# Gated cross-attention block: the rounded numbers of batch 6 transposed on TensorE, batch 7's sums and tokens kept elsewhere, 88 idle transposes

## The chip, the cores and the metric

The kernel runs on one core of one Trainium2 chip. The metric is the device time in microseconds (us), median of several runs; lower is better. The kernel before takes 510.13 us (three runs, 509.61 to 510.55).

## The reference

For each of 8 batches of 512 tokens by 256 channels (all float32):

```python
a   = layernorm(x)                                  # batch b
emb = a + ctx
q, k, v = emb @ wq + bq, emb @ wk + bk, emb @ wv + bv
w   = pos_bias * (|i - j| < 64)                     # 512 x 512, near the diagonal
ek, ew = exp(k - max_k), exp(w - max_w)
y   = sigmoid(q) * (ew @ (ek * v)) / (ew @ ek)
n1  = layernorm(y @ wo + bo + emb) * gamma + beta
n2  = layernorm(relu(n1 @ w1 + b1) @ w2 + b2 + n1) * gamma + beta
x1  = x + tanh(g_xattn) * n2
n3  = layernorm(x1)
xq  = round(n3 * 127 / max|n3|)                     # per token, then scaled back
h   = silu(xq @ Wg) * (xq @ Wu)                     # Wg, Wu, Wd rounded to -1, 0, 1 times a scale
out = x1 + tanh(g_ffn) * (round(h * 127 / max|h|) @ Wd)
```

The hidden width of both feed-forward parts is 1024.

## The kernel before, in words

One function writes a separate instruction list for each engine, by hand, with a semaphore count for every kind of step. Tokens of a batch lie as 4 tiles of 128; `b` is the batch, `t` a token tile, `p` a pair of tiles, `m` one of 8 slices of the hidden width. The batches are staged: while TensorE does the attention of batch b+1 it also does the first feed-forward part of batch b (`hidden`, `feed_forward`) and the rounded part (`gate`, `up`, `down`) of batch b-1. Each engine runs its list in order, and a step whose semaphore isn't there holds all behind it.

Float32 products are made of three TensorE products of rounded halves (`product`, L2502): high by high, high by low, low by high. So between two products ScalarE rounds the high half (`..._upper`) and VectorE subtracts to get the low one (`..._lower`). The table `BANK` says which of the 8 PSUM banks each step of each batch writes; `bank_wait` makes TensorE wait for the last reader of what was in that bank before. `gate` and `up` take two neighbouring banks.

The start. TensorE waits for the identity and then runs `WARM_UP` idle transposes into bank 7 (L2690), then `emb_rows(0, ...)` (L2510, transposes of the embedded tokens, after GpSimd's `embed`, L564), `keys_T` (L2519), `queries`, `keys_values`, the transposed positions (L2469), `attend` (L2562), `key_sums` (L2571) and `attend_far` (L2579). VectorE's list there holds `wkv_lower` (L1518), `emb_lower` (L1609), `key_max` (L1616), `position_max`, `add_bias`, `weighted` (L1644) and `e_lower` (L1649). After `attend_far(0, ...)` come `beta_w1` and `emb_rows(1, 0)`, which waits for bank 7 until VectorE's `b1_whole` (L1567), behind the divisions of batch 0 (`inverse`, L1658).

The rounded part of a batch. For each pair of tiles: GpSimd's `rsqrt` (L554 to L559), ScalarE's `normalise(b, 3, p)` (L870), VectorE's `token_max` (L1711) and `token_scales` (L1719, L1723), ScalarE's `token_quantise` (L943). The rounded tokens must be transposed: for most batches ScalarE writes them as bf16 (`xq_whole`, L961) and SyncE's queue issues a DMA transpose (`xq_rows`, L345). For the batches in `PE_BATCHES`, batch 7 alone, TensorE transposes float16 halves of the same words (`xq_rows`, L2643) and ScalarE copies them out of PSUM (`xq_columns`, L969). Then `gate` and `up` on TensorE (L2662), `silu` on ScalarE (L977), `product` (L1732) and `product_scale` (L1738 to L1750) on VectorE, `quantise` on GpSimd for even tiles (L608, L609) and on ScalarE for odd ones (L982). The rounded products are transposed in the same two ways: `hq_whole` (ScalarE, L999) with a DMA transpose (L352), or TensorE's `hq_rows` (L2652) with ScalarE's `hq_columns` (L990). Then `down` on TensorE (L2684) and `output` on VectorE (L1756), and SyncE stores pairs of tiles (L331).

The sum x1 has one home for all batches, `x1`, and `n3` and the results share `out_t`. So GpSimd's `first_sum(7, p)` (L603) waits for outputs of batch 6, which still read x1. `second_residual` (L1705) adds the result of the first feed-forward part; batch 7 alone does that part in two halves of tokens (`HALVED`: `hidden(7, m, p, HALF[p])`, `feed_pair`), and `second_residual(7, 1)` needs `feed_pair(7, 7, 1)`. The waits of the sums and tokens stand in `first_sum`, `normalise` and `output`.

Of the kernel before, what the change touches and what calls it, by code (L numbers as in the profile page):

```python
# [30 lines left out]
WARM_UP = 50  # L31

PE_BATCHES = (7,)
# [15 lines left out]
    ("embT", 0): (0, 7, 6, 5, 0, 4, 0, 4), ("embT", 1): (1, 3, 7, 0, 7, 6, 7, 6), ("kT", 0): (2, 1, 1, 5, 3, 3, 3, 0),  # L49
# [3 lines left out]
    ("num", 0): (1, 6, 5, 3, 3, 3, 3, 0), ("den", 0): (6, 4, 0, 0, 4, 0, 4, 6), ("num", 1): (3, 3, 1, 7, 6, 7, 6, 1),  # L53
# [31 lines left out]
def flamingo_layer(nc, x, ctx_in, g_xattn, g_ffn, wq, bq, wk, bk, wv, bv, wo, bo, pos_bias, gamma, beta,  # L85
                   w1, b1, w2, b2, w_gate, w_up, w_down, out):
    with ExitStack() as stack:
# [700 lines left out]
        def _(act):  # L788
# [74 lines left out]
            def normalise(b, n, p):  # L863
# [3 lines left out]
                if n == 3:  # L867
                    wait(act, out_stored[p], b, 0)
# [2414 lines left out]
```

## Time and profile before

| | |
|---|---|
| median of 3 runs | 510.13 us (509.61 to 510.55) |
| the profiled execution | 511.8 us, of which its span (first to last instruction) 509.8 us |
| TensorE busy | 480.8 us, 94% of the span |
| VectorE busy | 437.8 us, 86% |
| ScalarE busy | 375.3 us, 74% |
| GpSimd busy | 248.2 us, 49% |
| mean granted TensorE clock | 0.968 of full |
| chain that ended last | TensorE 86%, VectorE 5%, DMA 3%, ScalarE 2% |

TensorE's records overlap, since matmuls are pipelined: a matmul of 128 x 256 shows 0.28 us, and 54 in a row take 6.36 us. So start to start is what counts, not the length of one record. Times in the rows are in us from the start of the span.

### The profile page before, as it was taken

How to read it: one execution, taken by the hardware profiler on the slowest of the kernel's cores; microseconds unless marked ns; L12 is line 12 of the kernel's file. 1: busy time of each engine (PE TensorE's matmuls, PEld its weight loads, DVE VectorE, ACT ScalarE, POOL GpSimd, SP SyncE). 2: the span in 40 equal slices, each digit the busy share in tenths (PEclk: the TensorE clock that was granted, in tenths of full speed). 3: DMA queues.
4: the chain of work that ended last, by engine and by line, in shares of the span. 5: the costliest groups of instructions: out<-in, count | busy, mean ns of one | idle time of the engine just before them, and what ended most of it. 6: DMA issues, size and time to landing. Idle time of an engine off the chain costs nothing.

```text
span 509.8 us, 9743 instructions
## 1 busy us (share of the span) xinstructions
PE 480.8 (94%) x3010; PEld 397.1 (78%) x3010; DVE 437.8 (86%) x1002; ACT 375.3 (74%) x611; POOL 248.2 (49%) x389
## 2 busy tenths in 40 slices
PE   6898999999999999999999999999999999899483
PEld 6687888988877987788877987788878987787242
DVE  6889988786989899898989898999899888769574
ACT  3474869957778788696878688687768596898573
POOL 7292364169234493248525474339225903664511
PEclk9797999999999999999999999999999999999588
DMA  5853252222202331222312330223023101532301
GB/s 185 187 207 125 42 166 84 41 44 84 62 1 53 78 108 35 42 63 73 95 21 63 89 99 1 44 62 113 13 42 84 54 12 22 82 74 52 82 1 42
DMA packets 69329, 36.02 MB, mean 71 GB/s; under 512 B 47008, under 2 KB 68768, under 8 KB 69280
## 3 DMA queue, kind: packets, MB, share of 16 engines
q1 hardware_dynamic: 68448, 35.41, 27.5%
q8 instruction: 25, 0.41, 0.3%
q14 instruction: 24, 0.20, 0.1%
q10 hardware_dynamic: 832, 0.00, 0.1%
HBM read 20.46 MB, written 4.19 MB: 48 GB/s over the span
## 4 chain that ended last, share of the span: by engine, by line
PE 86%; DVE 5%; DMA 3%; ACT 2%; issue 2%; POOL 1%; SPq 0%; DVEq 0%; POOLq 0%; ACTq 0%
PE ps L2502 52%; PE ps L2662 10%; PE ps L2562 9%; PE ps L2684 5%; PE ps L2571 3%; PE ps L2519 2%; PE ps L2510 2%; DMA work<-in_L_xattn_wo_dram 2%; DMA w_bit<-place_c 1%; DVE cols L1738 1%; PE ps L2579 1%; PE ps L2597 1%; DVE work L1732 1%; PE ps L2536 1%; DVE ps L1658 1%
## 5 line engine op out<-in xcount | busy, mean ns | idle before, releaser
L554 POOL TENSOR_TENSOR mv<-mv,cols 128x2 f32<-128x2 f32 x64 | 13.1, 204 | 169.5 <-DVE mv L1604 169.3
L2502 PE MATMUL ps<-w_hi,h_hi 128*128 128x256 f32 x256 | 76.0, 297 | 0.0
L2502 PE MATMUL ps<-w_lo,h_hi 128*128 128x256 f32 x256 | 71.5, 279 | 0.0
L2502 PE MATMUL ps<-w_hi,h_lo 128*128 128x256 f32 x256 | 71.5, 279 | 0.0
L931 ACT ACTIVATE h_hi<-ps,cols 128x512 fp32r<-128x512 f32 (+1 forms) x72 | 45.4, 636 | 12.4 <-PE ps L2502 11.3
L2502 PE MATMUL ps<-n1T_hi,w_hi 128*128 128x512 f32 (+1 forms) x144 | 54.1, 376 | 0.4 <-DVE n1T_lo L1687 0.3
L1658 DVE RECIPROCAL ps<-ps 128x512 f32<-128x512 f32 x16 | 53.7, 3358 | 0.2 <-PE ps L2579 0.2
L2502 PE MATMUL ps<-n1T_hi,w_lo 128*128 128x512 f32 (+1 forms) x144 | 53.3, 370 | 0.0
L2502 PE MATMUL ps<-n1T_lo,w_hi 128*128 128x512 f32 (+1 forms) x144 | 53.3, 370 | 0.0
L2502 PEld LDWEIGHTS ps<-w_hi,h_hi 128*128 128x128 f32 x256 | 48.3, 189 | 3.0 <-DVE h_lo L1693 0.3
L977 ACT ACTIVATE work<-ps,cols 128x1024 f32<-128x1024 f32 x32 | 35.6, 1113 | 20.1 <-DVE work L1732 10.2
L2502 PEld LDWEIGHTS ps<-w_lo,h_hi 128*128 128x128 f32 x256 | 48.3, 189 | 1.1
L1693 DVE TENSOR_TENSOR h_lo<-ps,h_hi 128x512 fp32r<-128x512 f32 (+1 forms) x72 | 43.6, 622 | 5.9 <-ACT ps L936 5.2
L2502 PEld LDWEIGHTS ps<-w_hi,h_lo 128*128 128x128 f32 x256 | 48.2, 188 | 0.0
L2684 PE MATMUL ps<-wdT,w_bit 128*128 128x256 bf16 x256 | 35.9, 287 | 11.5 <-DMA w_bit<-place_c 7.5
L870 ACT ACTIVATE work<-work,nmr,rstd 128x256 f32<-128x256 f32 x64 | 34.8, 592 | 14.3 <-POOL nmr L559 14.3
L557 POOL TENSOR_TENSOR rstd<-mv,cols 128x2 f32<-128x2 f32 x64 | 45.0, 704 | 0.0
L936 ACT ACTIVATE ps<-ps,cols 128x512 f32<-128x512 f32 (+1 forms) x72 | 43.7, 611 | 0.0
L1732 DVE TENSOR_TENSOR work<-work,ps 128x1024 f32<-128x1024 f32 x32 | 38.9, 1215 | 4.9 <-PE ps L2662 3.1
L1596 DVE BATCH_NORM_STATS2 st<-work 128x6 f32<-128x256 f32 x96 | 36.1, 413 | 5.8 <-POOL work L603 5.5
L2684 PEld LDWEIGHTS ps<-wdT,w_bit 128*128 128x128 bf16 x256 | 24.0, 102 | 21.5 <-DMA w_bit<-place_c 10.8
L1738 DVE TENSOR_REDUCE cols<-work 128x1 f32<-128x1024 f32 x32 | 38.7, 1210 | 0.3
(179 smaller groups left out, 1480.6 us busy)
## 6 DMA issues: line engine op xcount, KB each, us to landing
x_in<-in_x_dram SPq DMA_DIRECT2D x16, 256.0 KB, 2.8
emb<-in_ctx_dram SPq DMA_DIRECT2D x16, 256.0 KB, 2.9
work<-in_x_dram SPq DMA_DIRECT2D x8, 512.0 KB, 4.0
out_dram<-work SPq DMA_DIRECT2D x16, 256.0 KB, 2.2
work<-in_L_xattn_w_dram SPq DMA_DIRECT2D x2, 1024.0 KB, 8.7
work<-in_L_ffn_w_gate_dram SPq DMA_DIRECT2D x1, 1024.0 KB, 5.7
work<-in_L_ffn_w_up_dram SPq DMA_DIRECT2D x1, 1024.0 KB, 5.7
place_c<-in_L_ffn_w_down_dram SPq DMA_DIRECT2D x1, 1024.0 KB, 9.0
```

Of the source, the lines that this page charges most:

```text
L557: pool.tensor_tensor(rstd[:, n, c], mv[:, n, c, 1], minus_half[:, c], ALU.pow).then_inc(power_step[n].sem, 1)
L931: nc.scalar.activation(h_hi[:, m % RING, c], h_bank(b, m, p)[:, c], ACT.Relu, bias=b1_col[:, m:m + 1]).then_inc(h_hi_ok.sem, 1)
L936: nc.scalar.activation(h_bank(b, m, p)[:, c], h_bank(b, m, p)[:, c], ACT.Relu, bias=b1_col[:, m:m + 1]).then_inc(h_relu_ok.sem, 1)
L1596: nc.vector.bn_stats(st6[:, n, t, :], src[:, t, :]).then_inc(stats[n].sem, 1)
L1658: nc.vector.reciprocal(bank(b, "den", h), bank(b, "den", h)).then_inc(rden_ok.sem, 1)
L1693: nc.vector.tensor_tensor(h_lo[:, m % RING, c], h_bank(b, m, p)[:, c], h_hi[:, m % RING, c], ALU.subtract).then_inc(h_lo_ok.sem, 1)
L1732: nc.vector.tensor_tensor(prod[t % 2].rearrange("p (a n) -> p a n", a=2), sg.rearrange("p (a n) -> p a n", a=2), bank_pair(b, "up", t), AL ...
L1738: nc.vector.tensor_reduce(hm[:, t:t + 1], prod[t % 2], AX.X, ALU.max, apply_absolute_value=True).then_inc(hm_ok.sem, 1)
L2502: last = nc.tensor.matmul(dst, lhsT, rhs, start=(i == 0 and not begun), stop=(i == n - 1 and ends))
L2562: nc.tensor.matmul(dst, lhsT[:, j, c], rhs[:, j, 0:n], start=(i == 0 and j == 0), stop=False, skip_group_check=True)
L2662: last = nc.tensor.matmul(dst[:, c, :].rearrange("p (j n) -> p j n", n=P), xqT[:, t, k, :], w[:].rearrange("p (j k) n -> p j k n", k=ND)[: ...
L2684: last = nc.tensor.matmul(bank(b, "down", t)[:, 0:D].rearrange("p (k n) -> p k n", n=P), hqT[t % 2][:, k, :], wdT[:].rearrange("p (k j) n ...
```

## The change

1. `WARM_UP` goes from 50 to 88, so 38 more idle transposes of the identity stand before `emb_rows(0, 0)`.
2. `PE_BATCHES` goes from (7,) to (6, 7). Batch 6's two `xq_rows` and four `hq_rows` leave SyncE's queue and become TensorE transposes (2 x 4 and 4 x 8); `xq_whole` and `hq_whole` become `xq_columns` and `hq_columns`.
3. Batch 7's x1 lives in `x_in`, its n3 in `emb`. So `first_sum(7, p)` waits for `emb_ok` instead of batch 6's outputs, and `output(7, t)` waits for the store of batch 6. The wait of `hout` for outputs of the batch before is by tile.
4. The lists of batches 6 and 7 get a new order on all engines, and some steps of batches 0 to 5 change place. `beta_w1` is cut in four pieces, called one after another.
5. A new `BANK` table.

```diff
-WARM_UP = 50
-PE_BATCHES = (7,)
+WARM_UP = 88
+PE_BATCHES = (6, 7)
...
+        def sum_of(b):
+            return x_in if b == NB - 1 else x1
+        def n3_of(b):
+            return emb if b == NB - 1 else out_t
...
             def first_sum(b, p):
...
-                wait(pool, out_ok, b, 2 * p - 2)
-                pool.tensor_tensor(half(x1, p), half(n2, p), half(xb, p), ALU.add).then_inc(x1_ok.sem, 1)
+                if b == NB - 1:
+                    wait(pool, emb_ok, b, 2)
+                else:
+                    wait(pool, out_ok, b, 2 * p - 2)
+                pool.tensor_tensor(half(sum_of(b), p), half(n2, p), half(xb, p), ALU.add).then_inc(x1_ok.sem, 1)
...
-                wait(dve, out_ok, b, 0)
+                wait(dve, out_ok, b, t - NT + 1)
...
+                if b == NB - 1:
+                    wait(dve, out_stored[t // 2], b, 0)
```

SyncE's list loses `xq_rows(6, 0)`, `xq_rows(6, 1)` and `hq_rows(6, 0)` to `hq_rows(6, 3)`. On GpSimd `rsqrt(7, 2, 0)` now stands before `quantise(6, 0)`, and `quantise(6, 2)` after `first_sum(7, 1)`. The end of TensorE's new list:

```diff
+            xq_rows(6, 0)
             hidden(7, 3, 1, HALF[1])
             hidden(7, 4, 1, HALF[1])
             feed_pair(7, 7, 0)
+            hidden(7, 5, 1, HALF[1])
             feed_pair(7, 0, 1)
             gate(6, 0)
+            hidden(7, 6, 1, HALF[1])
+            hidden(7, 7, 1, HALF[1])
+            feed_pair(7, 1, 1)
             up(6, 0)
...
+            xq_rows(6, 1)
             feed_pair(7, 2, 1)
             feed_pair(7, 3, 1)
...
+            gate(6, 1)
             feed_pair(7, 4, 1)
+            feed_pair(7, 5, 1)
             gate(6, 2)
...
             feed_pair(7, 6, 1)
+            hq_rows(6, 0)
+            feed_pair(7, 7, 1)
             gate(6, 3)
             down(6, 0)
...
+            up(6, 1)
+            up(6, 2)
+            up(6, 3)
+            hq_rows(6, 1)
             down(6, 1)
+            hq_rows(6, 2)
+            xq_rows(7, 0)
             down(6, 2)
...
             gate(7, 0)
+            hq_rows(6, 3)
             up(7, 0)
             gate(7, 1)
             up(7, 1)
+            down(6, 3)
             xq_rows(7, 1)
```

VectorE's new list from there: `second_residual(7, 1)`, `tile_stats` (7,3,0), (7,2,2), (7,2,3), (7,3,1), `mean_variance(7, 2, 1)`, `output(6, 0)`, `mean_variance(7, 3, 0)`, `product(6, 1)` with its scale, `product(6, 2)`, `token_max(7, 0)`, `product_scale(6, 2)`, `token_scales(7, 0)`, `product(6, 3)`, `tile_stats(7, 3, 2)`, `product_scale(6, 3)`, `output(6, 1)`, `tile_stats(7, 3, 3)`, `mean_variance(7, 3, 1)`, `output(6, 2)`, `token_max(7, 1)`, `token_scales(7, 1)`, `product(7, 0)` with its scale, `output(6, 3)`, `product(7, 1)`; from there as before.

## Rows read from the trace of the kernel before

**Rows 1.** Stretches: busy (instructions) of TensorE, its loads, VectorE, ScalarE, GpSimd; granted clock, DMA.
```profile
10.00:20.00 10.00, 4.96 (x15) 4.01 (x16) 6.56 (x8) 5.11 (x9) 3.65 (x6) 0.66 0.81 195
...
240.00:250.00 10.00, 10.00 (x68) 9.05 (x67) 9.97 (x17) 9.07 (x19) 6.31 (x4) 1.00 0.43 118
...
470.00:480.00 10.00, 4.00 (x24) 2.45 (x23) 7.11 (x21) 6.77 (x10) 7.24 (x13) 0.70 0.44 96
480.00:490.00 10.00, 7.95 (x31) 3.11 (x28) 4.98 (x16) 6.04 (x13) 2.46 (x5) 0.62 0.08 28
```

**Rows 2.** The chain that ended last, its pieces: start, us, what.
```profile
442.27 6.36 PE ps L2502 x54
...
455.15 1.74 PE ps L2662 x8
...
476.35 3.04 DMA w_bit<-place_c
```

**Rows 3.** The idle transposes, grouped, in the stretches 1.6 to 5 and 7 to 9.6.
```profile
L2690 PE MATMUL ps<-ident 128*128 128x128 f32 x16 | 3.7, 421 | 1.6 <-POOL ident L617 1.6
...
L2690 PE MATMUL ps<-ident 128*128 128x128 f32 x24 | 2.8, 273 | 0.0
```

**Rows 4.** TensorE in order of time at the start (idle time before it, releaser).
```profile
1.61 8.00 PE L2690 MATMUL ps<-ident 128*128 128x128 f32 x50 [1.61 <-POOL ident L617]
14.35 1.94 PE L2510 MATMUL ps<-ident,emb 128*128 128x128 f32 x8 [4.74 <-POOL emb L564]
16.98 2.07 PE L2519 MATMUL ps<-embT_hi,wkv_hi 128*128 128x512 f32 x4 [0.69 <-ACT embT_hi L884]
...
44.27 1.94 PE L2510 MATMUL ps<-ident,emb 128*128 128x128 f32 x8 [1.24 <-DVE cols L1567]
```

**Rows 5.** VectorE in order of time at the start.
```profile
16.96 0.69 DVE L1609 TENSOR_TENSOR embT_lo<-ps,embT_hi 128x512 fp32r<-128x512 f32 x1 [0.16 <-ACT embT_hi L884]
...
19.09 0.69 DVE L1616 TENSOR_REDUCE cols<-ps 128x1 f32<-128x512 f32 x1 [0.16 <-PE ps L2519]
...
27.60 0.76 DVE L1644 TENSOR_TENSOR ps<-ps,kv_f 128x256 f32<-128x256 f32 x2 [0.62 <-ACT ps L897]
...
32.72 1.28 DVE L1649 TENSOR_TENSOR e_lo<-ps,e_hi 128x512 fp32r<-128x512 f32 x2
```

**Rows 6.** TensorE in order of time near the end.
```profile
470.22 0.28 PE L2502 MATMUL ps<-w_hi,h_lo 128*128 128x256 f32 x1
...
475.45 1.89 PE L2684 MATMUL ps<-wdT,w_bit 128*128 128x256 bf16 x8 [2.94 <-DMA w_bit<-place_c]
...
489.47 0.38 PE L2643 MATMUL ps<-ident_h,work 128*128 128x128 f16 x4 [0.20 <-DVE work L1732]
493.10 0.61 PE L2652 MATMUL ps<-ident_h,work 128*128 128x128 f16 x8
```

**Rows 7.** VectorE, GpSimd, then ScalarE, in order of time near the end.
```profile
483.38 0.75 DVE L1596 BATCH_NORM_STATS2 st<-work 128x6 f32<-128x256 f32 x2 [1.54 <-POOL work L603]
487.03 0.69 DVE L1711 TENSOR_REDUCE cols<-work 128x2 f32<-128x512 f32 x1 [2.51 <-ACT work L870]
...
488.11 1.22 DVE L1732 TENSOR_TENSOR work<-work,ps 128x1024 f32<-128x1024 f32 x1
...
491.32 1.21 DVE L1732 TENSOR_TENSOR work<-work,ps 128x1024 f32<-128x1024 f32 x1
...
482.02 1.27 POOL L603 TENSOR_TENSOR work<-work 128x512 f32<-128x512 f32 x1 [2.40 <-DVE work L1756]
...
490.57 0.67 ACT L969 ACTIVATE xqT<-ps,cols 128x512 bf16<-128x512 f16 x1
...
494.76 1.23 ACT L982 ACTIVATE work<-work,cols 128x1024 f32<-128x1024 f32 x1
```

**Rows 8.** Shorter stretches, columns as in rows 1.
```profile
474.00:476.00 2.00, 0.55 (x3) 0.43 (x4) 1.36 (x7) 1.97 (x2) 1.45 (x3) 0.51 0.78 199
...
488.00:490.00 2.00, 1.65 (x10) 0.56 (x8) 1.97 (x3) 1.80 (x5) 0.00 (x0) 1.00 0.00 0
```

More of the change, by code:

```diff
@@ L504, in _ @@
             store(5, 1)
-            xq_rows(6, 0)
             fetch_x_again(7)
-            xq_rows(6, 1)
-            hq_rows(6, 0)
-            hq_rows(6, 1)
-            hq_rows(6, 2)
             store(6, 0)
-            hq_rows(6, 3)
             store(6, 1)
@@ L772, in _ @@
             x_beta(7)
+            rsqrt(7, 2, 0)
             quantise(6, 0)
-            rsqrt(7, 2, 0)
-            quantise(6, 2)
             n2_gamma(7, 0)
@@ L781, in _ @@
             first_sum(7, 1)
+            quantise(6, 2)
             rsqrt(7, 3, 1)
@@ L863, in normalise @@
             def normalise(b, n, p):
-                dst, src = {0: (xn, x_in), 2: (n2, a2), 3: (n3, x1)}[n]
+                dst, src = {0: (xn, x_in), 2: (n2, a2), 3: (n3_of(b), sum_of(b))}[n]
                 wait(act, nmr_ok[n], b, p + 1)
-                if n == 3:
+                if n == 3 and b == NB - 1:
+                    wait(act, embT_ps, b, 2)
+                    wait(act, embo_ok, b, 1)
+                elif n == 3:
                     wait(act, out_stored[p], b, 0)
@@ L1139, in _ @@
             normalise_tile(2, 1)
+            silu(0, 1)
             normalise_tile(2, 2)
-            silu(0, 1)
             normalise_tile(2, 3)
@@ L1421, in _ @@
             hidden_whole(6, 6)
+            silu(5, 0)
             hidden_upper(6, 7)
             hidden_whole(6, 7)
-            silu(5, 0)
             silu(5, 1)
@@ L1479, in _ @@
             hidden_whole(7, 5, 1, HALF[1])
+            xq_columns(6, 1)
             hidden_upper(7, 6, 1, HALF[1])
@@ L1483, in _ @@
             hidden_whole(7, 7, 1, HALF[1])
-            hq_whole(6, 0)
+            silu(6, 1)
+            normalise(7, 2, 0)
+            hq_columns(6, 0)
+            normalise(7, 2, 1)
             silu(6, 2)
+            normalise(7, 3, 0)
             quantise(6, 1)
-            hq_whole(6, 1)
             silu(6, 3)
-            normalise(7, 2, 0)
-            hq_whole(6, 2)
-            quantise(6, 3)
-            hq_whole(6, 3)
-            normalise(7, 2, 1)
-            normalise(7, 3, 0)
+            hq_columns(6, 1)
             product_scales(7, 0)
             token_quantise(7, 0)
+            hq_columns(6, 2)
+            quantise(6, 3)
             xq_columns(7, 0)
@@ L1499, in _ @@
             silu(7, 0)
+            hq_columns(6, 3)
             token_quantise(7, 1)
+            silu(7, 1)
             product_scales(7, 1)
-            silu(7, 1)
             xq_columns(7, 1)
@@ L1927, in _ @@
             weighted(2, 1)
+            weighted(2, 2)
             e_lower(2, 0)
-            e_lower(2, 1)
             hidden_lower(1, 0)
@@ L1932, in _ @@
             tile_stats(0, 3, 1)
+            e_lower(2, 1)
+            e_lower(2, 2)
             hidden_lower(1, 1)
@@ L1936, in _ @@
             tile_stats(0, 3, 3)
-            weighted(2, 2)
             mean_variance(0, 3, 1)
-            e_lower(2, 2)
             add_bias(2, 3)
@@ L2448, in _ @@
             product_scale(7, 0)
+            output(6, 3)
             product(7, 1)
@@ L2478, in far_row, with beta_w1 @@
                 last.then_inc(far_ps, 1)
-            def beta_w1():
+            def beta_w1(piece):
                 pe.wait_ge(load["vectors2"], 16 * VECTORS2)
                 pe.wait_ge(load["w1"], 16)
-                once_bank_wait(B1_BANK, (b1_ok, 1))
-                for m in range(NH):
+                if piece == 0:
+                    once_bank_wait(B1_BANK, (b1_ok, 1))
+                for m in range(2 * piece, 2 * piece + 2):
                     for k in range(ND):
@@ L2728, in _ @@
             attend_far(0, "num", 1)
-            beta_w1()
+            for piece in range(4):
+                beta_w1(piece)
             emb_rows(1, 0)
```

211 lines of the change are left out of this document (99 added, 112 removed), and 22 rows, old and new, of the table BANK.

## The prediction

> **What bounds the kernel now.** I read the stretches of 10 us first, then the chain, then each engine in order of time at the start and at the end. In the steady part TensorE is busy all the time at the full clock, with VectorE close behind [rows 1]. There an order can only save the few tenths that TensorE idles. Two places are not like that. Between 10 and 20 us TensorE is busy 4.96 of 10 us at a mean clock of 0.66, and between 470 and 490 it is busy 12.0 of 20 us at 0.70 and 0.62 [rows 1]. At the end the chain runs through a DMA transpose of 3.04 us [rows 2], GpSimd's first_sum, which waited 2.40 us for VectorE's output [rows 7], and then VectorE's products, one each 3.21 us (488.11 to 491.32) [rows 7]. So the time is: a start, a TensorE stretch of some 430 us, and a tail of waits between VectorE, ScalarE and GpSimd.
>
> **The start: 38 more idle transposes.** The 50 run from 1.61 to 9.61. The first 16 records have a mean of 421 ns, the last 24 of 273 ns, at 2.8 us for 24, or 0.117 each [rows 3, 4]. So 38 more take 4.4 us, and end at 14.0 to 14.1. The first real transposes begin at 14.35, held by GpSimd's embed [rows 4]; nothing waits for TensorE before that. The filler costs nothing, with 0.3 us to spare.
>
> What it changes is the clock. After the idle 4.74 us the eight transposes take 1.94 us and the four key products 2.07 [rows 4], all at the lower level of 1.2 GHz; the mean clock of that stretch is 0.66 [rows 1]. Without the gap they run at 2.4 GHz: half of each, 0.97 and 1.03. TensorE itself wins about 1.0 + 1.0 + 0.6 (three query products) = 2.6 us. VectorE can't follow in full. embT_lo (16.96) waits for ScalarE's copy, and two maxima of about 0.6 follow, of which the last starts at 19.09 now and could start at 17.7 [rows 5]: 1.4 us earlier. Later there is one wait of 0.62 us for ScalarE's exponentials (27.60) [rows 5], which follow TensorE's transposed positions. With TensorE 2.4 us ahead it falls to almost nothing, so VectorE is 1.9 to 2.0 us ahead when e_lower(0, 3) ends, at 34.0 now [rows 5]. key_sums, which needs it, follows 0.4 us later now, so TensorE gains 2.0 to 2.3. I take 2.1. Bounds: 1.2 if a load of x or of the positions lands too late, 2.6 if VectorE never holds TensorE. The stop before 44.27 (1.24 us, for VectorE's b1) and the slow clock behind it [rows 4] stay, since bank 7 and the order of b1 are the same. The 2.1 us reach the end, because all up to 470 us hangs on TensorE.
>
> Here a rule of the skill speaks against the change. The Trainium skill (TensorE: Matmul & The Clock Gate, Part 4: PE-mode transpose) says that transposes don't count as work for the clock gate. By that rule the extra transposes would leave the start as it is. The trace shows the clock's rise, from 421 to 273 ns, in a stretch with nothing but these transposes [rows 3], so it disagrees; the rule is the rival "no clock" below.
>
> **The middle: batches 0 to 5.** The moved attends, projections and lowers keep their number. TensorE is busy 10.00 of 10 us [rows 1], so I cost them at nothing, between a gain of 0.5 and a loss of 0.5 for the new banks.
>
> **The tail, TensorE.** Now feed_pair(7, 7, 1) ends at 470.50 [rows 6]. Six products of its kind take 0.70 us (54 in 6.36), a gate or up 0.87 (two in 1.74) [rows 2]. The new list moves gate(6, 3), down(6, 0), up(6, 1), up(6, 2) and up(6, 3) behind it, 5 x 0.87 = 4.35, and puts in two xq_rows of 0.38 and one hq_rows of 0.61 [rows 6]: 1.37. It ends at 470.5 - 4.35 + 1.37 = 467.5, if no step before it waits. gate(6, 0), up(6, 0), gate(6, 1) and gate(6, 2) now share banks 6 and 7, so each waits for the silu or product of the one before. Laid out with these durations, each is there 0.3 to 0.6 us before TensorE asks. Six DMA transposes, 3.04 us from issue to landing [rows 2], become 0.38 or 0.61 us of TensorE and a copy of 0.67 us (xq) or about 1.1 (hq) on ScalarE [rows 7] in place of its bf16 write of about the same length. So ScalarE's load doesn't change.
>
> **The tail, VectorE.** second_residual(7, 1) can start at 467.5. Now VectorE is busy 7.11 + 4.98 = 12.1 us between 470 and 490 [rows 1]. Less 1.1 of product(6, 3) ahead of second_residual and 1.9 of product(7, 0) behind 488.11, 9.1 us of work lie between second_residual(7, 1) and product(7, 0). The new list adds product(6, 1) and product(6, 2) with their scales, 2 x 3.21, and product(6, 3), 1.2, which stood before it; output(6, 0) comes in and output(6, 3) goes behind, which cancels. 9.1 + 7.6 = 16.7. Without a wait product(7, 0) would start at 484.2. One wait is left. From the first of two statistics to token_max is 3.65 us now (483.38 to 487.03) [rows 7], with one statistic 3.3. VectorE fills 1.1 of that (statistic, aggregate, output(6, 2)), and 2.2 us stay idle. So product(7, 0) starts at 486.4, against 488.11. Then come 3.21 us and output(6, 3), 0.4, and product(7, 1) starts at 490.0 against 491.32 [rows 7]: 1.3 us. From there both kernels run the same list, 18.5 us to 509.8.
>
> first_sum(7, 1) no longer waits for batch 6's outputs (2.40 us now [rows 7]); it ends near 475, with room, and what is late next is the pair's last statistic, behind product_scale(6, 3). The new wait of output(7, t) for a store has some 10 us to spare. SyncE's queue only loses steps. GpSimd's quantise(6, 2) now stands behind first_sum(7, 1), which is done before its factor is there.
>
> **The sum.** 511.8 - 2.1 - 1.3 = 508.4 for the profiled execution; the median of the runs is 1.7 lower, so 510.13 - 3.4 = 506.7.
>
> **The rivals.**
> "Slow tail". The clock fell at about 474 and was back by 488 [rows 8], after idle stretches of 2.94 us and the like [rows 6]. The new list is idle too, between up(6, 3) at 472.2 and hq_rows(6, 1) at 475.3. If the clock is still low at 483, this decides: the factor of tile 3 at 481.4, quantise 1.23, xq_columns 0.67 [rows 7], to 483.3; then gate, hq_rows and up, 2.35 at full, 4.7 at half clock, to 488.0 instead of 485.7. product(7, 0) starts at 488.0 and product(7, 1) at 491.7 to 492.0, a loss of 0.5: 510.13 - 2.1 + 0.5 = 508.5. For it: the idle stretch. Against it: from 477.5 on TensorE would be nearly dense, and after 44.27 and after 14.35 a dense stretch brought the clock back [rows 1, 4]. Chance 0.24.
>
> "No clock". The start's gain is missing, since transposes don't hold the clock or don't fill the gap: 510.13 - 1.3 = 508.8. The records at 273 ns speak against it [rows 3]. Chance 0.05.
>
> "Stall in the shared banks", slower than before. Between 456 and 467 TensorE's list is one line through banks 6 and 7 and through two transposes of tokens that need VectorE's scale. If VectorE or ScalarE run 0.6 us later than laid out, each of xq_rows(6, 1), gate(6, 1), gate(6, 2) and hq_rows(6, 0) waits. When they sum to more than 3.4 us the change loses. With four waits of 1 us and the clock fallen for the last 3 us of work ahead of 467.5, it is +4.0 + 3.0 - 3.4 + 510.13 = 513.7. Against it: the margins above, and the kernel's like waits of 0.1 to 0.3 us. Chance 0.07.
>
> A last case is that small waits everywhere eat most of the gain: 509.1 to 511, 0.10.
>
> **How the numbers follow.** Forecast 506.7 with chance 0.54, its own range 504.8 to 508.2 (start 1.2 to 2.6, middle and banks 0.5 each way, tail 0 to 2.5). The range that holds 8 in 10 takes in "slow tail" and "no clock" and a little of the last case, and below a tail in which VectorE finds all its work ready: 504.6 to 509.2. A difference of 0.2%, 1.0 us, is about what a measurement of this kernel can tell from none. Faster by more (below 509.1): 0.54 + 0.24 + 0.05, less a little: 0.82. Within: 0.11. Slower: 0.07.
>
> **What would show it.** Transposes without a gap from 1.6 to about 14.1, and eight real ones in 0.97 us; key_sums and the stop before emb_rows(1, 0) 2 us earlier; feed_pair(7, 7, 1) ending at 465.4 on the new time axis (467.5 less 2.1); product(7, 0) near 484.3 and product(7, 1) near 487.9; the clock back at 1.00 before gate(7, 0). The prediction is wrong if TensorE waits by name for silu or product between 454 and 466, if the middle gives back the start's gain, or if VectorE's idle time before product(7, 0) is above 5 us.

## The result, and the profile after

The changed kernel takes 508.95 us (median of 20 runs, 507.68 to 509.71), the kernel before 512.26 us (median of 20, 509.60 to 513.55). The ratio of their runs is 0.9945, with a 95% interval of 0.9933 to 0.9958. So the change saves 2.8 us (2.1 to 3.4); the two medians lie 3.3 us apart, and the text goes by the ratio. In another set of runs beside the experiments below the ratio was 0.9958 (0.9941 to 0.9974). The profiled execution took 509.66 us with a span of 507.9, against 511.8 and 509.8 before.

The stretches of the changed kernel, with the columns of [rows 1]: length, busy time (instructions) of TensorE, its weight loads, VectorE, ScalarE, GpSimd, then granted clock, DMA share, GB/s.

```profile
10.00:20.00 10.00, 7.79 (x51) 6.47 (x50) 7.72 (x12) 5.60 (x10) 3.69 (x6) 1.00 0.77 196
...
280.00:290.00 10.00, 9.15 (x69) 8.31 (x69) 7.60 (x22) 5.49 (x12) 3.24 (x6) 1.00 0.44 57
340.00:350.00 10.00, 8.95 (x62) 7.94 (x62) 7.17 (x22) 4.85 (x10) 5.85 (x9) 1.00 0.58 101
470.00:480.00 10.00, 5.55 (x36) 3.31 (x34) 9.62 (x22) 7.98 (x13) 5.36 (x10) 0.78 0.00 0
480.00:490.00 10.00, 8.50 (x45) 4.72 (x44) 6.03 (x19) 8.66 (x13) 1.30 (x5) 0.70 0.07 26
```

Between 10 and 20 us the clock is 1.00 instead of 0.66 [rows 1]. In the tail TensorE is busier than before, at 0.78 and 0.70. New are two places in the middle, 280 to 290 and 340 to 350 us: TensorE is busy 9.15 and 8.95 us of 10 there, and was 9.97 and 10.00 before.

TensorE in order of time at the start, to be read beside [rows 4]:

```profile
1.61 11.29 PE L2704 MATMUL ps<-ident 128*128 128x128 f32 x88 [1.61 <-POOL ident L625]
14.38 1.07 PE L2524 MATMUL ps<-ident,emb 128*128 128x128 f32 x8 [1.48 <-POOL emb L569]
16.18 1.19 PE L2533 MATMUL ps<-embT_hi,wkv_hi 128*128 128x512 f32 x4 [0.74 <-ACT embT_hi L895]
...
42.07 1.84 PE L2524 MATMUL ps<-ident,emb 128*128 128x128 f32 x8 [1.23 <-DVE cols L1578]
```

The 88 transposes ended at 12.90 instead of 9.61, 3.3 us later, and left 1.48 us idle. From start to start a transpose takes 0.213 us at 1.2 GHz and 0.109 at 2.4 GHz in both traces. In the kernel before the clock came up at 6.4 us, here at 4.7, so part of the longer row was made up by the clock. It stayed up over the 1.48 us: eight real transposes take 1.07 us instead of 1.94, and the stop of batch 1 ends at 42.07 instead of 44.27 [rows 4], 2.2 us earlier.

Then the chain that ended last, in the middle (start us, us, what; L1010 is ScalarE's hq_whole, L2698 down, L2585 key_sums):

```profile
280.11 1.07 ACT place_c L1010
281.18 0.02 issue
281.19 4.56 DMA w_bit<-place_c
285.76 0.05 issue
285.81 1.05 PE ps L2698 x8
286.85 1.87 PE ps L2585 x8
...
338.62 4.79 DMA w_bit<-place_c
343.40 0.04 issue
343.45 1.05 PE ps L2698 x8
```

Two DMA transposes land 4.56 and 4.79 us after their issue, where 3.0 is usual, and TensorE stands idle 0.82 and 1.05 us ahead of down(2, 3) and down(3, 3). That is the most of what the two stretches above lack.

The tail on VectorE (second_residual(7, 1), an output of batch 6, token_max(7, 1), product(7, 0)):

```profile
466.97 0.69 DVE L1716 TENSOR_TENSOR work<-ps,work 128x512 f32<-128x512 f32 x1 [2.80 <-PE ps L2516]
...
482.80 0.48 DVE L1769 SCALAR_TENSOR_TENSOR work<-ps,cols,work 128x256 f32<-128x256 f32 x1 [1.41 <-PE ps L2698]
483.91 0.69 DVE L1722 TENSOR_REDUCE cols<-emb 128x2 f32<-128x512 f32 x1 [0.63 <-ACT emb L881]
...
486.64 1.22 DVE L1743 TENSOR_TENSOR work<-work,ps 128x1024 f32<-128x1024 f32 x1 [1.59 <-PE ps L2676]
```

and on TensorE (L2666 hq_rows, L2698 down, L2676 gate and up):

```profile
474.79 0.62 PE L2666 MATMUL ps<-ident_h,work 128*128 128x128 f16 x8 [2.73 <-ACT work L993]
476.88 1.87 PE L2698 MATMUL ps<-wdT,w_bit 128*128 128x256 bf16 x8 [1.47 <-ACT w_bit L1001]
...
480.90 1.86 PE L2698 MATMUL ps<-wdT,w_bit 128*128 128x256 bf16 x8 [0.87 <-ACT w_bit L1001]
482.60 1.86 PE L2676 MATMUL ps<-wgT,xqT 128*128 128x512 bf16 x4
484.26 1.06 PE L2666 MATMUL ps<-ident_h,work 128*128 128x128 f16 x8
485.12 1.43 PE L2676 MATMUL ps<-wuT,xqT 128*128 128x512 bf16 x4
...
503.71 1.03 PE L2698 MATMUL ps<-wdT,w_bit 128*128 128x256 bf16 x8 [1.30 <-ACT w_bit L1001]
```

No down of the tail waits for a DMA transpose any more ([rows 6] has 2.94 us of it). From 475.7 to 485.9 TensorE is at 1.2 GHz: gate(7, 0) takes 1.86 us, and product(7, 0) waits 1.59 us for up(7, 0) though VectorE has the tokens' scales at 485.05. The last down, at 503.71, runs at 2.4 GHz (1.03 us); before it took 1.87.

### The profile page after: what moved, and what is told of

It reads as the page before. It is cut to its first block, busy times and chain, and to the rows that moved or that the text cites. A ratio compares the mean times of both kernels' runs of the same rounds, so it can differ in the third digit from the quotient of the medians.

```text
span 507.9 us, 9896 instructions
## 1 busy us (share of the span) xinstructions
PE 483.6 (95%) x3088; PEld 400.6 (79%) x3088; DVE 437.5 (86%) x1002; ACT 374.5 (74%) x611; POOL 248.6 (49%) x389
## 4 chain that ended last, share of the span: by engine, by line
PE 76%; ACT 8%; DVE 6%; DMA 5%; issue 3%; POOL 1%; SPq 0%; DVEq 0%; ACTq 0%; POOLq 0%
PE ps L2516 47%; PE ps L2676 8%; PE ps L2576 7%; PE ps L2698 4%; DMA w_bit<-place_c 3%; PE ps L2585 3%; PE ps L2533 2%; DMA work<-in_L_xattn_wo_dram 2%; PE ps L2524 2%; DVE cols L1749 1%; PE ps L2593 1%; ACT place_c L1010 1%; DVE work L1743 1%; PE ps L2611 1%; ACT work L993 1%
## 5 line engine op out<-in xcount | busy, mean ns | idle before, releaser
L559 POOL TENSOR_TENSOR mv<-mv,cols 128x2 f32<-128x2 f32 x64 | 13.2, 206 | 162.6 <-DVE mv L1615 162.4
L2698 PE MATMUL ps<-wdT,w_bit 128*128 128x256 bf16 x256 | 35.0, 282 | 9.2 <-ACT w_bit L1001 6.3
L881 ACT ACTIVATE work<-work,nmr,rstd 128x256 f32<-128x256 f32 x60 | 32.7, 594 | 14.2 <-POOL nmr L564 14.1
L2698 PEld LDWEIGHTS ps<-wdT,w_bit 128*128 128x128 bf16 x256 | 23.8, 100 | 18.8 <-ACT w_bit L1001 7.2
L1607 DVE BATCH_NORM_STATS2 st<-work 128x6 f32<-128x256 f32 x92 | 34.6, 412 | 3.4 <-POOL work L611 3.2
```

The costliest lines, as they stand in the source:

```text
L2698: last = nc.tensor.matmul(bank(b, "down", t)[:, 0:D].rearrange("p (k n) -> p k n", n=P), hqT[t % 2][:, k, :], wdT[:].rearrange("p (k j) n ...
```

## The experiments

Theories after the first comparison. A, for the middle: the late transposes are set by something other than the order of the work. B, for the middle: ScalarE's new order (exp_keys(b, 2) ahead of hq_whole(b - 3, 3) in batches 3 to 6) makes the fourth transpose late. C, for the start: 2.1 us that reach the end. D, for the tail: the slow clock takes back a part.

To place the gains, four times are read in every trace: the starts of key_sums of batches 3 and 6 (TensorE), of second_residual(7, 1), and of product(7, 0) and product(7, 1) (VectorE). "n" is what the edits at the start and at the stop of batch 1 add to TensorE's instructions; an idle transpose counts as two, its weight load and its matmul (three more waits in the changed kernel's new order are left out). "Late" are the DMA transposes of rounded products that took 4.1 us or more, by time of issue. The trace of keys_tail is at a mean clock of 0.943 (tail_filled 0.986), so its times are not compared with the others'. The ratio's interval stands with each experiment.

| kernel | n | key_sums 3 to 6 | late | residual (7, 1) | to product(7, 0) | product(7, 1) to end | ratio to before |
|---|---|---|---|---|---|---|---|
| before | 0 | 168.6 | 382.1, 436.9 | 471.36 | 16.75 | 18.48 | 1 |
| start_alone | 76 | 169.9 | 280.7, 337.7 | 469.99 | 16.74 | 17.86 | 0.9962 |
| changed | 76 | 171.3 | 281.2, 338.6 | 466.97 | 19.67 | 17.65 | 0.9945 |
| after_again | 76 | 170.7 | 281.8, 319.0 | 466.97 | 18.05 | 18.88 | 0.9958 |
| start_undone | 0 | 169.3 | 385.1 | 468.81 | 19.37 | 17.62 | 0.998 |
| tail_filled | 76 | 170.4 | 210.6, 280.9, 317.9 | 466.03 | 18.02 | 19.15 | 0.9947 |
| fetch_moved | 120 | 171.5 | 172.1, 229.5, 286.6, 343.7 | 471.91 | 19.29 | 17.70 | 1.0053 |
| before_76_waits | 76 | 169.8 | 283.1, 339.9 | 472.32 | 16.74 | 18.53 | 1.0043 |
| stop_filled | 108 | 171.2 | 169.4, 226.7, 283.7, 340.8 | 468.84 | 18.05 | 19.00 | 0.9987 |
| keys_back | 76 | 170.4 | 280.5, 337.8 | 465.95 | 18.02 | 18.73 | 0.9940 |
| wide_start | -8 | 169.4 | 436.0 | 466.82 | 18.05 | 18.93 | 0.9948 |
| keys_tail | 76 | 171.0 | 281.1, 338.6 | 467.01 | 18.10 | 18.09 | 0.9908 |
| all_three | -8 | 168.6 | 380.4, 434.7 | 465.54 | 18.02 | 17.94 | 0.9897 |
| all_three_b2 | 20 | 168.6 | 380.7 | 464.41 | 18.03 | 17.96 | 0.9873 |
| all_three_again | -8 | 168.6 | 380.1, 434.4 | 465.11 | 18.03 | 17.96 | 0.9894 |

### The start alone, and the change without it

```diff
-WARM_UP = 50
+WARM_UP = 88
```

> The kernel before with 88 idle transposes in place of 50, nothing else. Theory 'the start pays in full': clock 1.00 through 10 to 20 us, key_sums of batch 0 at about 32.5 instead of 34.57, the stop before emb_rows(1, 0) ends at 42.1 instead of 44.27, and the whole is 2.1 us faster, a ratio of 0.9959. Rival 'the lead is lost': TensorE's 2 us of lead make it wait for VectorE, ScalarE or the transposes later, and less than 1.0 us reach the end, a ratio above 0.998.

Measured: 509.72 us against 511.87, a ratio of 0.9962 (0.9947 to 0.9978), 1.95 us. The clock is 1.00 from 10 to 20 us, key_sums(0) at 32.3. But the lead shrank to 1.4 us by second_residual(7, 1); two transposes were late that were not late before, and from key_sums(3) to (6) it took 1.3 us more.

For the changed kernel the edit the other way:

> The changed kernel with 50 idle transposes. If the start pays 2.1 to 2.2 us and the two parts add up, what is left of the 2.8 us is 0.6 to 0.7: a ratio of 0.9986 (0.998 to 0.9992). If the start pays nothing in the end, the ratio is that of the whole change, 0.9945. In the profile TensorE's stretch from 14.35 is at 1.2 GHz again and key_sums of batch 0 is at 34.6; the tail from second_residual(7, 1) on lasts as in the changed kernel, 40.9 us from its start to the end of the span.

Measured: 511.07 us, 0.998 (0.9957 to 1.0003), so 1.0 us are left, and the stretch from 10 to 20 us is back at a clock of 0.62. 1.95 and 1.0 add up to 2.95; the whole change gave 2.1 and 2.8 in its two sets. C holds within the intervals. It also means that all but the start is worth about 1 us, which these runs can't tell from nothing (the interval is 2.2 us to a loss of 0.2). Two things stand beside this number. The 12 runs fall apart: four took 508.2 to 508.4 us at a mean granted clock of 0.978, eight 510.7 to 512.6 at 0.963 to 0.976, so the median hangs on how many were of which kind. And key_sums(0) stood at 35.6 in the profile, not at the 34.6 expected; TensorE was at 1.2 GHz from 12.5 to 22.7 us there, and from 13.2 to 20.1 in the kernel before.

### The changed kernel once more

> The changed kernel once more, for a second profiled execution and for its time beside the others on one chip. Theory 'chance in the middle': the two late DMA transposes of batch 2 and 3 (4.56 and 4.79 us to landing instead of 3.0, with TensorE idle 0.82 and 1.05 us behind them) are an accident of that execution. Then in this one they land at other places or nowhere, the key_sums of batch 6 starts 1 to 2 us earlier than 344.50, and the profiled gain over the kernel before is nearer to 3. Rival 'order of the middle': ScalarE's exp_keys ahead of hq_whole makes the fourth transpose of batches 0 to 3 late every time, so down(2, 3) and down(3, 3) wait 0.8 to 1.0 us again. Time under both: ratio to the kernel before 0.993 to 0.996.

Measured: 509.29 us, 0.9958 (0.9941 to 0.9974), span 507.5. One of the two late transposes was the same (281.8), the other had moved from batch 3's fourth tile to its first (319.0). So neither expectation is right as put: it is not an accident that falls anywhere, and not the order alone. What settles it is the DMA queues in a window of 6 us around such a transpose. First the kernel before (281 to 287), then the changed one (280 to 286):

```profile
q1 hardware_dynamic: 1056, 0.26, 22.7%
issues: line engine op xcount, KB each, median us to landing
w_bit<-place_c SPq DMA_TRANSPOSE x1, 3.0
```

```profile
q1 hardware_dynamic: 1056, 0.26, 57.2%
q8 instruction: 1, 0.02, 1.0%
issues: line engine op xcount, KB each, median us to landing
w_bit<-place_c SPq DMA_TRANSPOSE x1, 4.6
```

A single packet of some 16 KB on queue q8 fell into the flight of the transpose, whose own packets (1056 in both) then took 57.2% of the window instead of 22.7%. The rates of that window show how: once begun the transpose moves 171 to 205 GB/s until 283.15, then for 1.5 us 10 at most, and the rest in a burst. The packet began at 283.0. In the kernel before 190 to 225 GB/s go on without a break. The queue is named "instruction" by the profile. It has 25 packets in the whole kernel before (0.41 MB) and 26 in the changed one (0.43 MB). Most come 12 to 25 us apart, on average one for 232 matmuls and weight loads of TensorE, or for 256 of its records with the waits counted in (254 in the changed kernel). Over the 15 traces of the table I took the transposes of rounded products of batches 0 to 5, 24 in each or 360, with their time to landing, and the packets. 32 were late, and each of the 32 has a packet that began 1.00 to 2.13 us behind its issue. No other transpose has a packet in that place. With one up to 0.98 us behind the issue they landed in 3.0 to 3.7 us (3.71 at 0.98, in all_three_b2), with one from 2.50 us on in 3.0 to 3.1. The Trainium skill (Perfetto Trace Analysis, Per-instruction lifecycle: The 4-stage abstract model) says that an instruction has 64 bytes; a packet of 16 KB would be 256 of them, and the traces agree with their 254 to 256 records.

### Only the instructions, not the transposes

before_76_waits puts into the kernel before 152 waits for const_ok, long met, which make 76 instructions:

```diff
+            for _ in range(40):
+                pe.wait_ge(const_ok, 5)
             for _ in range(WARM_UP):
                 nc.tensor.transpose(ps[:, 7, 0:P], ident[:], ident[:])
+            for _ in range(112):
+                pe.wait_ge(const_ok, 5)
```

> The kernel before with 76 more such instructions (as many as 38 idle transposes have, matmul and weight load each) but no transpose more, all in the idle stretches ahead of 14.35. The start keeps its slow clock. Theory 'instruction fetch': the packets come as in start_alone, near 283 + 2 and 338 + 2 us, the fourth transposes of batches 2 and 3 land in 4.3 to 4.8 us, from key_sums of batch 3 to that of batch 6 it takes 169.9 us instead of 168.59, and the kernel is 0.5 to 1.5 us slower than before. Rival 'nothing but chance': it is within 0.3 us of the kernel before.

Measured: 513.73 us, 1.0043 (1.0026 to 1.006), 2.2 us slower. The fourth transposes of batches 2 and 3 landed after 4.3 and 4.5 us, and from key_sums(3) to key_sums(6) it took 169.8 us (169.9 expected). Part of the loss is a cost that I had taken for nothing: each instruction takes 0.11 us even when its wait is met.

```profile
3.76 7.38 PE L2692 MATMUL ps<-ident 128*128 128x128 f32 x50 [3.76 <-issue]
15.17 1.94 PE L2510 MATMUL ps<-ident,emb 128*128 128x128 f32 x8 [4.02 <-issue]
```

20 of them hold the idle transposes to 3.76, and the real ones start at 15.17 instead of 14.35 [rows 4]. That is 0.8 us; the late transposes are 1.2 us, the rest of 2.2 is within the interval. TensorE ran 0.8 us late here and 2.1 us early in start_alone, and the same two transposes were late, so it is not its lead that makes them late.

### Moving the packets in the changed kernel

fetch_moved has 40 such waits ahead of the 88 transposes and 48 behind, 44 instructions.

> The changed kernel with 44 more instructions in TensorE's list that do nothing (waits for const_ok, long met): 20 ahead of the idle transposes, 24 behind them, in a stretch where TensorE waits anyway. Theory 'instruction fetch': queue q8 brings TensorE's instructions in packets of 16 KB, one for about every 230 matmuls and weight loads; a DMA transpose in flight when such a packet comes lands 1.3 to 1.8 us late. With 44 more instructions each packet comes some 2.8 us earlier against the work. The packets at 283.0 and 339.5 then fall to about 279.5 and 336.5, before the transposes of 281.2 and 338.6 are issued; these land in 3.0 us, down(2, 3) and down(3, 3) wait for nothing, key_sums of batch 6 starts 1.0 to 1.5 us earlier against key_sums of batch 3 than in the changed kernel (169.5 to 170.3 behind it instead of 171.28), and the kernel is 1.0 us faster than the changed one, if no packet hits another transpose without slack. Rival 'order of the middle': the waits are there as before, the time is the changed kernel's.

Measured: 514.02 us, 1.0053 (1.0033 to 1.0073). The expectation was wrong. The start lost 2.1 us (real transposes at 16.51), and the packets did not clear the transposes: they came 1.2 to 1.3 us behind the issue of the fourth one in all of batches 0 to 3 (1.8 and 1.3 in the changed kernel's two), and all four were late. So the number of instructions decides which transposes are hit, but my 2.8 us of shift was no good forecast of where the packets go.

stop_filled was made for another reason, to keep the clock up at the stop of batch 1:

```diff
+            idle(4, 10)
             emb_rows(1, 0)
             emb_rows(1, 1)
+            idle(4, 6)
```

(idle(place, n) waits for the last reader of that bank and makes n idle transposes.)

> The changed kernel with idle transposes at the stop of batch 1: 10 ahead of emb_rows(1, 0), 6 behind emb_rows(1, 1), in bank 4. Now TensorE waits 1.23 us there for VectorE's b1 and then works at 1.2 GHz from 42.3 to 49.0. Theory: the clock stays at 2.4 GHz; the keys and queries of batch 1 are held by VectorE's embT_lo (46.38) but run at full speed behind it, so that the first values of batch 1 come 1.3 us sooner, and as TensorE is dense from there the kernel gains 1.0 to 1.5 us over the changed one (ratio to the kernel before 0.992 to 0.9935), less or more what the 32 instructions do to the fetches. Rival 'VectorE holds the stretch' (it is busy 10.00 of 10 us there): TensorE's gain turns into waits for VectorE up to 60 us and less than 0.4 us is left.

Measured: 510.73 us, 0.9987 (0.997 to 1.0003), slower than the changed kernel. The clock between 40 and 50 us is 0.83 instead of 0.66, but TensorE now waits for VectorE's embT_lo and for a small step of the maxima, 0.3 us each, and key_sums(1) starts only 0.3 to 0.9 us earlier. The 32 instructions, though, made four transposes late, as in fetch_moved. VectorE holding the stretch is likely from this; it isn't shown by itself, since the packets moved too.

### The order of ScalarE's list

```diff
-            exp_keys(4, 2)
             hq_whole(1, 3)
             hidden_whole(3, 1)
+            exp_keys(4, 2)
```

and the same for batches 3, 5 and 6.

> The changed kernel with ScalarE's exp_keys(b, 2) of batches 3 to 6 behind hq_whole(b - 3, 3) and hidden_whole(b - 1, 1) again, as in the kernel before. The fourth transposes of batches 0 to 3 are then issued 0.3 us earlier. Theory 'instruction fetch': a packet can still hit them (283.0 lies in the flight of 280.9 to 283.9), so this changes the time by less than 0.3 us. Rival 'order of the middle': down(2, 3) and down(3, 3) wait no more and the kernel is 1 us or more faster than the changed one.

Measured: 508.22 us, 0.994 (0.9922 to 0.9958). Both late transposes are still there (4.8 and 4.7 us), so the order doesn't cause them. But where nothing is late a batch takes 0.3 us less: from key_sums(2) to (3) to (4) it takes 54.6 and 56.1 us, as before the change (54.6, 56.1), and 54.8 and 56.4 in every trace with the new order but fetch_moved and stop_filled, where a late one lies between. wide_start below, with the new order and no late one in these batches, has 54.8, 56.4, 56.4 and 56.6; all_three, with the old order and no late one, has 54.6, 56.1, 56.1 and 56.4. So B holds in part, with 0.2 to 0.3 us for each of four batches, and the expected "less than 0.3 us" was too low: second_residual(7, 1) comes 1.0 us earlier than in the changed kernel.

### The same start with fewer instructions

wide_start replaces the 88 transposes by 8, and by 38 products of 512 columns, four times as wide:

```diff
-            for _ in range(WARM_UP):
+            for _ in range(8):
                 nc.tensor.transpose(ps[:, 7, 0:P], ident[:], ident[:])
+            pe.wait_ge(dve_const_ok, 5)
+            for _ in range(38):
+                nc.tensor.matmul(ps[:, 7, :].rearrange("p (k n) -> p k n", n=P), tile_ones[:, 0:P],
+                                 tile_ones[:, None, 0:P].to_broadcast([P, 4, P]), start=True, stop=True)
```

> The changed kernel with its 88 idle transposes replaced by 8 of them and 38 idle products of 512 columns (tile_ones by itself, four times as wide): the same stretch of TensorE's time with 92 instructions instead of 176. Theory 'instruction fetch': the clock is 1.00 from 10 to 20 us and key_sums of batch 0 stands at 32.4 as in the changed kernel, but the packets of queue q8 come as in start_undone, where no fourth transpose of batches 0 to 3 was late. So these land in 3.0 us, from key_sums of batch 3 to that of batch 6 it takes 169.3 us instead of 170.7 to 171.3, and the kernel is 1.2 to 1.8 us faster than the changed one: ratio to the kernel before 0.991 to 0.993. Rival 'the lead itself makes them late' (TensorE early against its queues, whatever the count): 170.5 or more as before, ratio 0.9945 to 0.9958.

Measured: 508.76 us, 0.9948 (0.993 to 0.9967). TensorE at the start:

```profile
1.61 1.97 PE L2704 MATMUL ps<-ident 128*128 128x128 f32 x8 [1.61 <-POOL ident L625]
3.23 10.04 PE L2707 MATMUL ps<-tile_ones 128*128 128x512 f32 x38
14.29 1.07 PE L2524 MATMUL ps<-ident,emb 128*128 128x128 f32 x8 [1.01 <-POOL emb L569]
```

No transpose of batches 0 to 4 is late, and from key_sums(3) to (6) it takes 169.4 us (169.3 expected). The start is as early as in the changed kernel (key_sums(0) at 32.3 in both), so the rival of the lead is out. The mechanism is as expected, the time is not: a packet met the transpose issued at 436.0 instead (4.5 us, TensorE idle 1.2 us), and the kernel is only as fast as the changed one.

### The tail

tail_filled puts idle transposes into TensorE's gaps behind up(6, 3), behind hq_rows(6, 1), before down(6, 2) and before gate(7, 0):

```diff
             up(6, 3)
+            idle(7, 17)
             hq_rows(6, 1)
+            idle(7, 11)
             down(6, 1)
             hq_rows(6, 2)
             xq_rows(7, 0)
+            idle(7, 8)
             down(6, 2)
+            idle(7, 12)
             gate(7, 0)
```

> The changed kernel with idle transposes of f32 in TensorE's gaps of the tail: 17 behind up(6, 3), 11 behind hq_rows(6, 1), 8 before down(6, 2), 12 before gate(7, 0), all in a bank whose last reader is done. Theory 'slow tail': the clock stays at 2.4 GHz, gate(7, 0), hq_rows(6, 3) and up(7, 0) are over by 484.6 on the changed kernel's axis, product(7, 0) starts when VectorE has the tokens (485.05) instead of 486.64, and the whole is 1.2 to 1.6 us faster than the changed kernel (ratio to the kernel before 0.9915). Rival 'ScalarE sets the tail': quantise and the copies behind it come no sooner, product(7, 0) moves by less than 0.4 us, ratio 0.9938 to 0.9945. Rival 'the filler is in the way': a transpose of the rounded numbers or a down waits for the filler, and the kernel is slower than the changed one.

Measured: 508.71 us, 0.9947 (0.9929 to 0.9965). The clock is 1.00 from 470 to 490 us, and product(7, 0) starts 18.02 us behind second_residual(7, 1) instead of 19.67. But the total is only 0.6 us below after_again beside it. The traces say why. In after_again the clock came back by itself, at 480.3, while in the changed kernel's first profile it came back at 485.9; from second_residual(7, 1) at 466.97 up to 480.9 all engines stand at the same times to 0.01 us in both:

```profile
476.88 1.86 PE L2698 MATMUL ps<-wdT,w_bit 128*128 128x256 bf16 x8 [1.47 <-ACT w_bit L1001]
...
480.89 1.03 PE L2698 MATMUL ps<-wdT,w_bit 128*128 128x256 bf16 x8 [0.87 <-ACT w_bit L1001]
482.59 1.02 PE L2676 MATMUL ps<-wgT,xqT 128*128 128x512 bf16 x4 [0.67 <-ACT xqT L980]
...
502.51 1.87 PE L2698 MATMUL ps<-wdT,w_bit 128*128 128x256 bf16 x8 [1.30 <-ACT w_bit L1001]
```

down(6, 2) takes 1.03 us here and 1.86 there. product(7, 0) starts at 485.02, 1.6 us earlier. But then the last down is at 1.2 GHz. This trade is in the table: where the clock was back by 483 or never fell (after_again, tail_filled, stop_filled, keys_back, wide_start) product(7, 0) comes 18.0 us behind the residual and the end 18.7 to 19.2 us behind product(7, 1); where it came back at 486 or later (the changed kernel, start_undone, fetch_moved) it is 19.3 to 19.7 and 17.6 to 17.7. The two together (with 3.6 us between the products) come to 40.3 to 40.9 us in all eight. Why an early return goes with a fall at the end is not shown. And no trace has less than the 18.0: with TensorE at full clock VectorE waits for ScalarE's tokens, as the last row shows (tail_filled, VectorE before token_max(7, 1)).

```profile
482.97 0.69 DVE L1722 TENSOR_REDUCE cols<-emb 128x2 f32<-128x512 f32 x1 [2.15 <-ACT emb L881]
```

### All together

keys_tail is keys_back with tail_filled and with idle(1, 9), idle(1, 9), idle(1, 4) and idle(1, 10) before down(7, 1), down(7, 2), hq_rows(7, 3) and down(7, 3).

> The changed kernel with keys_back, with the idle transposes of tail_filled, and with 9, 9, 4 and 10 more in bank 1 in TensorE's gaps before down(7, 1), down(7, 2), hq_rows(7, 3) and down(7, 3), so that the last down runs at 2.4 GHz every time. The start and so the phase of the fetches is the changed kernel's: two late transposes, 170.4 us from key_sums of batch 3 to that of batch 6. If the parts add up: 0.8 (keys) + 0.6 (tail) + 0.4 (end, half of 0.85) = 1.8 us faster than the changed kernel, ratio 0.9915. If the tail's chain of ScalarE and VectorE takes it back: 0.993.

Measured: 506.98 us, 0.9908 (0.9881 to 0.9935). That is about the 0.9915 expected if the parts add up. The last down takes 1.05 us. Its two late transposes are the changed kernel's. With TensorE filled at both places the trade is gone: from second_residual(7, 1) to the end it is 39.8 us here (at the mean clock of 0.943) and 39.6 in the three traces below.

> wide_start and keys_tail together. If late transposes are a matter of TensorE's count of instructions, from key_sums of batch 3 to that of batch 6 it takes 168.6 us as in the kernel before (undisturbed landings and ScalarE's old order), and the whole is 1.2 to 1.8 us faster than keys_tail: ratio 0.988 to 0.990. If not, it is as keys_tail.

Measured: 506.84 us, 0.9897 (0.9872 to 0.9923), 168.6 us from key_sums(3) to (6) as expected. The gain over keys_tail is 0.1 us by medians, not 1.2 to 1.8: the packets hit transposes at 380.4 and 434.7 instead.

all_three_b has 36 transposes and 24 wide products at the start, 28 instructions more.

> all_three with another mix at the start: 36 idle transposes and 24 wide products, 120 instructions instead of 92, in the same time. In all_three one packet of queue q8 (435.5) still met a transpose without slack (issued at 434.7, landed after 4.6 us, TensorE idle 1.3 us) and one met that of 380.4. Theory 'instruction fetch': 28 instructions more move the packets 1.5 to 2.0 us earlier against the work. The ones at 435.5 and 381.5 then come before the issues at 434.7 and 380.4, while those at 285.5 and 342.0, which stood 5 us behind the issues of the fourth transposes of batches 2 and 3 (280.5, 336.8), stay just clear of their 3.0 us in flight. TensorE's wait at 434.7 goes, second_residual(7, 1) starts near 464.4 instead of 465.54, and the kernel is 0.8 to 1.3 us faster than all_three (ratio 0.9875). If the packets don't move like that, another transpose is late and the time is all_three's or up to 1.5 us more.

Measured: 505.86 us, 0.9882 (0.9856 to 0.9908). Its trace can't be laid beside the others: each matmul takes more than twice as long in it all the way (the eight real transposes 2.64 us instead of 1.07), and its span is 1236.7 us. The same kernel again, and all_three beside it:

> all_three_b once more, for a trace of it. Instruction fetch: the packets that stood at 435.5 and 381.5 in all_three come 1.5 to 2.0 us earlier against the work, all DMA transposes of batches 0 to 5 that have no slack land in 3.0 to 3.5 us, TensorE doesn't wait 1.3 us near 436, and second_residual(7, 1) starts near 464.4. If it is not the fetch, the transpose at 434.7 is late again, and this kernel is no faster than all_three beside it.

> all_three once more, beside all_three_b2 on one chip. The transposes issued at 380.4 and 434.7 are late again (4.3 and 4.6 us) and no other, 168.6 us from key_sums of batch 3 to that of batch 6, second_residual(7, 1) near 465.5; ratio to the kernel before 0.9897, 0.8 to 1.3 us above all_three_b2. If late landings were mere chance they would be at other places.

Measured: 505.78 us, 0.9873 (0.9852 to 0.9895), and 506.86 us, 0.9894 (0.9868 to 0.9919). all_three's late transposes came back at the same places (380.1 and 434.4). In all_three_b2 the one at 435.0 landed in 3.0 us and second_residual(7, 1) started at 464.41 (464.4 expected). Queue q8 and the landing between 434 and 439, all_three_again and then all_three_b2:

```profile
q8 instruction: 1, 0.02, 1.5%
issues: line engine op xcount, KB each, median us to landing
out_dram<-work SPq DMA_DIRECT2D x1, 256.0 KB, 3.1
w_bit<-place_c SPq DMA_TRANSPOSE x1, 4.4
```

```profile
q8 instruction: 1, 0.02, 2.3%
issues: line engine op xcount, KB each, median us to landing
out_dram<-work SPq DMA_DIRECT2D x1, 256.0 KB, 4.4
w_bit<-place_c SPq DMA_TRANSPOSE x1, 3.0
```

The packet is in both, but at 435.9 in the one, 1.5 us behind the issue, and at 438.3 in the other, 3.3 us behind it, when the transpose had landed. I had expected it earlier, not later, and the one at 380.7 stayed late. all_three_b2 is the fastest version found: 1.3% below the kernel before.

## Why the prediction was right or wrong

Faster, as forecast, but by 2.8 us (2.1 to 3.4) and not by 3.4, and to 508.95 us, not 506.7. Three terms were off, in the order of their size. The one that fails the prediction's account of the change itself is the second, the middle costed at nothing.

**The base of the sum.** I took the median to be 1.7 us below the profiled execution, from three runs with a median of 510.13. Over 20 runs the median before is 512.26; the profiled 511.8 was the better base. The spread goes with the clock: of the 24 runs of the kernel before beside the first experiments, the nine with a mean granted clock of 0.970 or more took 509.6 to 511.4 us, the 15 below took 511.2 to 513.6. 510.13 times the measured ratio is 507.3, so of the 2.25 us by which the forecast was too low 1.6 are the base and 0.6 the gain.

**"The middle costs nothing."** This is the step that failed on the kernel itself. I had 465.4 for the end of feed_pair(7, 7, 1); it ended at 466.86, and second_residual(7, 1), which follows it, started at 466.97, 1.6 us late. Against the kernel before, the stretch from key_sums(0) to key_sums(7) lost 2.8 us, with the one attend that changed sides counted in: 1.3 in differences of 0.1 to 0.3 for each batch, of which ScalarE's order is 1.1 at most, and 1.9 from the two late transposes; the last batch gave back 0.4. Then 1.2 more came back before 448 us (down(5, 3) at 447.96 against 448.47, from 0.7 behind at key_sums(7)), mostly since the transpose that was late in the kernel before at 436.9, with TensorE idle 0.96 us ahead of a down, wasn't late now. So TensorE was 0.5 us ahead there, not 2.1, and the middle cost 1.6 us. That was one of the signs I had named ("if the middle gives back the start's gain"), and it showed. I had seen that every transpose takes 3.04 us and took that as fixed, while two of the kernel before already took 4.4 and 4.3. And I took added instructions at the start to have an effect at the start only.

**The end.** From product(7, 1) I had 18.5 us to the end in both kernels; it is 17.65 or 18.9, depending on whether the clock is up at the last down.

What held: the start (2.2 us measured at the stop of batch 1, 2.1 forecast; 1.95 us timed alone). The filler cost nothing and kept the clock, though my price of 0.117 us for a transpose was too high: it is 0.109 at 2.4 GHz. The rule of the skill that transposes don't count for the clock gate (the Trainium skill, TensorE: Matmul & The Clock Gate, Part 4: PE-mode transpose) is contradicted once more: start_alone adds nothing but transposes and lifts the mean clock of 10 to 20 us from 0.66 to 1.00. (The trace lists them as MATMUL; whether they ran in the mode that the page speaks of it doesn't tell.) The tail's count came out near, in part by luck: from the end of feed_pair(7, 7, 1) to product(7, 0) I had 484.3 - 465.4 = 18.9 us, 16.7 of work and 2.2 of waiting. From second_residual(7, 1) on it is 19.67 in the first profile (15.5 busy, 4.2 idle) and 18.05 in after_again (15.4 and 2.6). So the work was forecast 1.2 us too high, and the waiting too low. The 3.6 us from there to product(7, 1) are as forecast.

Of the rivals, "slow tail" happened as described in the profiled execution: the clock was low until 486, and product(7, 0) waited 1.59 us for up(7, 0). Its price was forecast too high, since I didn't see that the last down would run at the full clock in return. That its 508.5 us lies near the measured 508.95 is luck: it stands for a gain of 1.6 us from a base that was too low. For the same reason it says little that 508.95 lies inside the range (504.6 to 509.2). "No clock" and "stall in the shared banks" did not happen; between 454 and 467 no wait of TensorE is above 0.3 us. The sign of VectorE idle more than 5 us before product(7, 0) showed only if its wait ahead of second_residual(7, 1) is counted: 2.80 us there, and 3.63 in waits behind it (1.41 + 0.63 + 1.59), where 2.2 were forecast.

What stays open: where a packet of queue q8 will fall. Its link to late landings is shown by 32 of 32, and that TensorE's count of instructions moves it by before_76_waits and wide_start; the forecasts of how far it moves (fetch_moved) and of its direction (all_three_b) were wrong. How much of the 1 us beside the start is due to what (TensorE's transposes instead of the DMA's, or the new homes of batch 7's sums) wasn't tried apart. Nor is it shown what sets the moment at which the clock comes back in the tail.

## What to carry to other kernels

Before costing a stretch at nothing because its engine is always busy, look at the longest landing in it, not the median, and at what waits for that transfer; then look in its window for a packet on an instruction queue. Adding or removing instructions on an engine, idle ones included, can change which transfers are late hundreds of microseconds on, so time any such edit in two or three counts before judging it. To fill a gap for the clock's sake few wide operations do as well as many small ones (38 products kept the clock at 1.00 as 80 transposes did) and bring fewer instructions; by itself this made no kernel here faster (wide_start 0.9948, the changed kernel 0.9945 and 0.9958).

## What was not expected of the hardware

- A packet of 16 KB on the instruction queue that begins 1.00 to 2.13 us behind the issue of a DMA transpose of 3.0 us makes it land after 4.1 to 4.8 us: 32 of 360, with no exception either way.
- The clock's return is not fixed by the program. In two executions of the same kernel, alike to 0.01 us from 466.97 up to 480.9, it was back at 2.4 GHz at 480.3 in one and at 485.9 in the other. The Trainium skill (TensorE: Matmul & The Clock Gate, Part 1: The HAM clock gate) says that the ramp at a kernel's start varies from run to run; these traces agree, with 14 idle transposes at 1.2 GHz in the changed kernel and 20 in after_again, the same kernel.
- A wait that is long met costs TensorE 0.11 us as an instruction of its own (20 in 2.15 us).
- The same 88 idle transposes end anywhere between 12.9 and 14.5 us in the seven traces that have them from 1.61 us on, with 14 to 28 of them at 1.2 GHz (0.213 us each, 0.109 at 2.4 GHz). The filler's length in one trace isn't its length in the next.
